# Band transposes of an attention kernel as 64-row halves, straight and crossed, among the row-tiled products

## The reference

```python
qkv = q @ in_proj_weight.T + in_proj_bias          # 16 heads of 16 features
scores = einsum('bhid,bhjd->bhij', qh / 4, kh)      # 1024 x 1024 for each head
rel = clip(pos[None, :] - pos[:, None], -64, 64) + 64
bias = take_along_axis(einsum('bhid,rd->bhir', qh / 4, rel_pe), rel)
attn = softmax(scores + bias)
x = layernorm(x + (attn @ vh) @ out_w.T + out_b)
x = layernorm(x + binarized_ffn(x))                 # 256 -> 1024 -> 256, exact gelu
```

## Time and profile before

| | us |
|---|---|
| median of 3 executions | 2435.11 (2433.6 to 2438.61) |
| the profiled execution | 2437.13 |
| its span, first to last instruction | 2435.4 |
| TensorE busy (products) | 2263.2, 93% of the span |
| VectorE busy | 1746.0, 72% |
| ScalarE busy | 1670.8, 69% |
| GpSimd busy | 966.1, 40% |

### The profile page before, as it was taken

How to read it: one execution, slowest core, us unless ns; L and a number is a source line. 1 busy time by engine, 2 the same in 40 slices (tenths; PEclk the granted TensorE clock), 3 DMA queues, 4 the chain that set the end, 5 groups by cost and what they waited for, 6 DMA issues and landing times. The chain is left out here.

```text
span 2435.4 us, 47764 instructions
## 1 busy us (share of the span) xinstructions
PE 2263.2 (93%) x14642; PEld 1272.1 (52%) x14642; DVE 1746.0 (72%) x3444; ACT 1670.8 (69%) x2239; POOL 966.1 (40%) x1565
## 2 busy tenths in 40 slices
PE   4998399999999999999999999999999999799997
PEld 3554144444444444444444444444444444688886
DVE  2454377777777777777777777777777773688885
ACT  2433157777777777777777777777777777466766
POOL 0000434444344443444334443444334432466663
PEclk9999579999999999999999999999999999899999
DMA  6998767777767777777777777777777762333311
GB/s 180 370 336 318 181 179 205 205 200 208 210 198 208 203 207 203 208 199 208 208 202 208 202 207 204 204 202 209 207 202 204 200 198 87 103 99 108 108 63 44
DMA packets 335292, 468.58 MB, mean 192 GB/s; under 512 B 90517, under 2 KB 263270, under 8 KB 335206
## 3 DMA queue, kind: packets, MB, share of 16 engines
q0 software_dynamic: 120960, 215.78, 35.0%
q1 hardware_dynamic: 201206, 243.05, 30.1%
q10 hardware_dynamic: 13040, 8.80, 1.2%
HBM read 244.73 MB, written 221.25 MB: 191 GB/s over the span
## 5 line engine op out<-in xcount | busy, mean ns | idle before, releaser
L896 ACT ACTIVATE probs<-weigh_ps 128x1024 f32<-128x1024 f32 x1024 | 1049.7, 1025 | 401.3 <-PE weigh_ps L1062 398.1
L1022 PE MATMUL ring_ps<-keys,queries 48*128 48x512 f32 x2048 | 839.3, 473 | 39.1 <-DVE partial_max L937 20.6
L948 DVE CUSTOM_DVE_ANT_1 ring_ps<-ring_ps,band_all 128x512 f32<-128x512 f32 x1008 | 681.0, 716 | 265.2 <-PE ring_ps L1022 265.0
L1062 PE MATMUL weigh_ps<-queries,keys 50*128 50x512 f32 (+3 forms) x2688 | 751.9, 385 | 1.4 <-ACT probs L896 0.8
L937 DVE TENSOR_REDUCE partial_max<-ring_ps 128x2 f32<-128x1024 f32 x512 | 627.9, 1226 | 165.7 <-PE ring_ps L1022 111.4
L1022 PEld LDWEIGHTS ring_ps<-keys,queries 48*128 48x128 f32 x2048 | 370.6, 187 | 517.9 <-issue 394.6
L1079 PE MATMUL sum_ps<-probs,values 128*32 128x512 f32 x4096 | 546.6, 605 | 0.1
L1047 PE MATMUL weigh_ps<-ident,band_all 128*128 128x128 f32 x2048 | 362.8, 290 | 22.8 <-ACT carried L884 20.2
L1062 PEld LDWEIGHTS weigh_ps<-queries,keys 50*128 50x128 f32 x2688 | 356.5, 186 | 17.7 <-ACT probs L896 9.5
L790 POOL DMA_DIRECT2D band_all<-band_scr x320 | 231.1, 725 | 332.9 <-DMA band_scr<-carried 318.3
L884 ACT ACTIVATE carried<-weigh_ps 128x512 f32<-128x512 f32 x512 | 302.6, 592 | 63.5 <-PE weigh_ps L1010 51.1
(11 more groups left out here) (115 smaller groups left out, 1858.6 us busy)
## 6 DMA issues: line engine op xcount, KB each, us to landing
band_scr<-carried SPq DMA_DIRECT2D x256, 512.0 KB, 4.0
band_all<-band_scr POOLq DMA_DIRECT2D x128, 512.0 KB, 6.6
band_all<-band_scr POOLq DMA_DIRECT2D x128, 256.0 KB, 3.3
keys<-k_scr POOLq DMA_DIRECT2D x128, 240.0 KB, 9.7
k_scr<-k_parts SPq DMA_DIRECT2D x16, 1792.0 KB, 8.4
q_scr<-q_parts SPq DMA_DIRECT2D x16, 1024.0 KB, 6.4
queries<-q_scr POOLq DMA_DIRECT2D x128, 128.0 KB, 2.9
o_scr<-weighted_s SPq DMA_DIRECT2D x64, 256.0 KB, 9.1
```

The source lines that it names most:

```text
L896: nc.scalar.activation(probs[:, u % PROBS], weigh_ps[weigh_of["scores", at]][:], ACT.Exp).then_inc(s_pr, 1)
L948: nc.vector.tensor_tensor_reduce(out=both, in0=both, in1=bias, scale=1.0, scalar=LOWEST, op0=ALU.add, op1=ALU.max, accum_out=partial_max[: ...
L1022: nc.tensor.matmul(dst, query_rows(c, h, ROWS, tile * P, (tile + 1) * P), key_rows(c, h, ROWS, c0, c0 + 512), start=True, stop=True, tile_ ...
L1062: last = nc.tensor.matmul(weigh_ps[weigh_of["scores", at]][:, h, e0 * P:e1 * P], key_rows(c, h, QROWS, k0, k0 + P), query_rows(c, h, QROWS ...
```

## The change

A tile of the band is no longer transposed with all 128 rows of the array, but in two halves of 64 rows (queries). The weights are 64 rows by 128 keys, the moving operand is 64 x 64 of the identity, and a half fills 64 of the 128 query columns. The array's rows 0 to 63 first take head 0's upper half while rows 64 to 127 take head 1's lower half ("straight"); then they swap heads ("cross"). The crossed ones wait on a semaphore for the straight ones, and the scores' products wait for the crossed ones. Each wait is followed by an instruction that increments a counter (`s_passed`). The order on TensorE becomes: looks (m, 0), weighs (m, 0), band product, weighted values, [turn of the maximum], straight (m, 1), looks (m, 1), cross (m, 1), straight of the next pair's part 0, weighs (m, 1), cross of the next pair's part 0. The two looks now stand together ahead of the weighs. ScalarE copies the turned maximum after the band instead of at the pair's start.

```diff
@@ ScalarE
                 def pair(i, step, m):
-                    if turns_at(step, 2 * m):
-                        copy_turned(i, turn_index(step, 2 * m))
                     if step >= 0:
                         expo(i, step, m, 0)
                     if m == 1 and step > 0:
                         copy_sums(i, step - 1)
                     if bands_at(step, m):
                         copy_band(i, band_index(step, m))
+                    if turns_at(step, 2 * m):
+                        copy_turned(i, turn_index(step, 2 * m))
                     if step >= 0:
                         expo(i, step, m, 1)
@@ TensorE
-                def turn_bands(i, c, m, part):
...
+                def turn_bands(i, c, m, part, cross):
+                    if not 0 <= c < G or not near(m, part):
+                        return
+                    n = weighed(m)[part] // 2
                     at = position(c, m, part)
+                    if cross:
+                        pe.wait_ge(s_straight, turns_before(i, c, m, part))
+                        pe.sem_inc(s_passed, 1)
+                    elif weigh_before["scores", at]:
+                        wait_for(i, weigh_before["scores", at])
+                        pe.sem_inc(s_passed, 1)
+                    for tile in near(m, part):
+                        side, e = (n - tile) % NT, tile % QT
+                        for r in range(HG):
+                            h, r0 = (1 - r if cross else r), r * ROW_TILE
+                            last = nc.tensor.matmul(
+                                weigh_ps[weigh_of["scores", at]][:, h, e * P + r0:e * P + r0 + ROW_TILE],
+                                band[r0:r0 + ROW_TILE, c % SLOTS, tile // 2, h, tile % 2, side * P:(side + 1) * P],
+                                ident[r0:r0 + ROW_TILE, r0:r0 + ROW_TILE], is_transpose=True,
+                                start=(not cross and tile == near(m, part)[0]), stop=False, skip_group_check=True,
+                                tile_position=(r0, 0))
+                            if tile == near(m, part)[-1]:
+                                last.then_inc(s_cross if cross else s_straight, 1)
...
+                def weighs_of(i, c, m, part):
...
+                    if near(m, part):
+                        pe.wait_ge(s_cross, turns_before(i, c, m, part))
+                    else:
+                        wait_for(i, weigh_before["scores", position(c, m, part)])
+                    for h in range(HG):
+                        weigh(c, m, part, h)
                 def pair(i, step, m):
-                    if turns_at(step, 2 * m):
-                        turn_max(i, turn_index(step, 2 * m))
-                    if step >= 0:
-                        turn_bands(i, step, m, 0)
-                    products(i, step, m, 0)
+                    following = (step, m + 1) if m + 1 < NT else (step + 1, 0)
+                    looks_of(i, step, m, 0)
+                    weighs_of(i, step, m, 0)
                     if bands_at(step, m):
                         band_product(i, band_index(step, m))
                     lagging(i, step, m)
-                    if step >= 0:
-                        turn_bands(i, step, m, 1)
-                    products(i, step, m, 1)
+                    if turns_at(step, 2 * m):
+                        turn_max(i, turn_index(step, 2 * m))
+                    turn_bands(i, step, m, 1, False)
+                    looks_of(i, step, m, 1)
+                    turn_bands(i, step, m, 1, True)
+                    turn_bands(i, *following, 0, False)
+                    weighs_of(i, step, m, 1)
+                    turn_bands(i, *following, 0, True)
```

More of the change, by code:

```diff
@@ L661, in post_ln_block @@
                     for u in (2 * m, 2 * m + 1):
-                        if turns_at(step, u):
-                            occupy(("turn", turn_index(step, u)), 1)
+                        if u % 2 and turns_at(step, u - 1):
+                            occupy(("turn", turn_index(step, u - 1)), 1)
                         if looks_at(step, u):
                             n = look_index(step, u)
-                            look_heads[n] = (1, 0) if u % 2 == 0 and (m % 2 == 0) != turns_at(step, u) else (0, 1)
+                            look_heads[n] = (1, 0) if u % 2 == 0 and (m % 2 == 0) != turns_at(step, u - 2) else (0, 1)
                             slots = LOOK_SLOTS[m % 2][u % 2]
@@ L1032, in turn_max @@
                                         ident[:]).then_inc(s_turn, 1)
-                def turn_bands(i, c, m, part):
-                    at = position(c, m, part)
-                    u = weighed(m)[part]
-                    n, g = u // 2, u % 2
-                    if u < 2:
-                        pe.wait_ge(s_min[g][c % SLOTS], i * (16 * HG) + 16 * HG * (c // SLOTS + 1))
-                    wait_for(i, weigh_before["scores", at])
-                    for h in range(HG):
-                        first = True
-                        for e in range(QT):
-                            tile = g * QT + e
-                            side = (n - tile) % NT
-                            if side < 2:
-                                nc.tensor.matmul(weigh_ps[weigh_of["scores", at]][:, h, e * P:(e + 1) * P],
-                                                 band[:, c % SLOTS, tile // 2, h, tile % 2, side * P:(side + 1) * P], ident[:],
-                                                 is_transpose=True, start=first, stop=False, skip_group_check=True)
-                                first = False
+                TURNED = [(0, 0), (0, 1), (1, 0), (2, 0), (3, 0), (4, 0), (4, 1), (5, 0), (6, 0), (7, 0)]
@@ new lines, in near, with turns_before @@
+                def near(m, part):
+                    n, g = weighed(m)[part] // 2, weighed(m)[part] % 2
+                    return [g * QT + e for e in range(QT) if (n - g * QT - e) % NT < 2]
+                def turns_before(i, c, m, part):
+                    return cnt(i, HG * len(TURNED), HG * (c * len(TURNED) + TURNED.index((m, part)) + 1))
+                def turn_bands(i, c, m, part, cross):
+                    if not 0 <= c < G or not near(m, part):
+                        return
+                    n = weighed(m)[part] // 2
+                    at = position(c, m, part)
+                    if cross:
[16 more added lines that the diff above has]
+                                last.then_inc(s_cross if cross else s_straight, 1)
@@ L1056, in weigh @@
                     tiles = range(g * QT, (g + 1) * QT)
-                    first = not any((n - t) % NT < 2 for t in tiles)
+                    first = not near(m, part)
                     rights = sum(1 for t in tiles if n > t + 1)
@@ L1089, in lagging, with looks_of @@
                         weighted(i, step - 1, NT - 2 + m)
[L1091 to L1109 removed]
+                def looks_of(i, step, m, part):
+                    if looks_at(step, 2 * m + part):
+                        n = look_index(step, 2 * m + part)
+                        for h in look_heads[n]:
+                            look(i, n, h)
+                def weighs_of(i, c, m, part):
+                    if c < 0:
+                        return
+                    g = weighed(m)[part] % 2
+                    if m == 0:
+                        pe.wait_ge(s_min[g][c % SLOTS], i * (16 * HG) + 16 * HG * (c // SLOTS + 1))
+                    if near(m, part):
[4 more added lines that the diff above has]
+                        weigh(c, m, part, h)
+                def pair(i, step, m):
+                    following = (step, m + 1) if m + 1 < NT else (step + 1, 0)
+                    looks_of(i, step, m, 0)
+                    weighs_of(i, step, m, 0)
                     if bands_at(step, m):
```

13 lines of the change are left out of this document (2 added, 11 removed).

## The result

The changed kernel takes 2816.0 us (median of 4, 2810.55 to 2817.14) where the kernel before takes 2436.32 (2433.6 to 2438.61). The ratio is 1.1546 [1.153, 1.1562], 380 us more. The sign was forecast, the size was not: 2816 lies far above the 2540 forecast and above the range. In what follows, one execution of e4 (2943.36 us) and one of e8 (3820.24 us, at a mean granted clock of 0.52) were slow ones and are outside the ratios; of e4's only steps at full clock are read.

A forecast was written before the change was run, and what follows sets the result against it. A loop through ScalarE, 3.17 us a pair, was taken as the bound. Pair terms, turns and increments gave 29.1 us a step against 27.47: +1.65 x 61 = +101 us on 2437.1, forecast 2540 us, range 2452 to 2630.

The forecast's parts named there:

- the clock: Rival, 3%: with TensorE waiting more, the clock could fall to half speed, some 2 us more per pair, far over 3000.
- pair 1 to 2: From weighted values of pair 1 to those of pair 2, weighs behind the band's copy: 4.33 us against 3.94.
- The halves' pace: Transposes by halves: a pair of halves side by side takes 0.055 us, against 0.105 for one full transpose.
- The third rival: Halves don't pair up, or their loads set the pace: 0.105 a pair, about 2570; one by one, 2666; chance 19%.
- From the second weigh to the exponential: Start of the second weigh to start of ScalarE's exponential, in every loop: 0.43 us.
- Increments: Counter increments behind the 20 waits per step: 0.1 us per step for those on the loops.
- The turn of the maximum: Moves from under ScalarE's work to between weighted values and looks, twice a step: 0.25 us each, 0.50 together.
- Plain pairs: Five pairs of a step without an extra: between 3.28 and 3.41 us, taken as 3.37, against 3.17 before.
- loop C: Loop over two pairs through look, weighs, band's copy, straight halves and part 1's exponential: 6.82 us, 3.41 a pair.
- The open pairs: Pairs 0 to 1 and 4 to 5: the full run's 0.37 goes, the longer loop stays; 3.67 us each.
- The "wrong if" list: Wrong if plain pairs repeat at 3.1 or less, band's copy ends well before straight halves, or their wait exceeds 0.1.
- TensorE's own work is the bound: Rival, 9%: TensorE's array time sets the pace, so halves save 3.2 us per step, giving 2242 us.

The follow-up runs named there:

- e4: Changed kernel with whole 128-row transposes in place of the straight halves, nothing for the crossed ones, no increments behind waits; 2850.05 and 2943.36 us, step 33.35.
- e8: Kernel before with TensorE's steps written out and the halves put into its old order of looks and weighs; 2571.28 us, ratio 1.0544.
- e1: Changed kernel with TensorE's steps written out, no loop on that engine; 2712.35 us, ratio 1.1133.
- e7: e1 with the looks of pair 1's second part done four times, filling a TensorE wait; 2603.08 us, ratio 1.0678.
- e6: e1 without the counter increments behind the waits for straight and crossed halves; 2667.26 us, ratio 1.0941.
- e9: e6 with the next pair's straight halves behind part 1's weighs, the crossed ones between the next pair's looks and weighs; 2652.3 us, ratio 1.0883.
- e12: Kernel before with ScalarE's copy of the sums moved from pair 1 to pair 2, behind the turned maximum's copy; 2417.93 us, ratio 0.9926.

## Why the prediction was wrong

**The sum of the 380 us, as measured.**

| term | from | us |
|---|---|---|
| longer step at full clock | (30.14 - 27.47) x 61 | 163 |
| stalls at the loop's turn | the row of waits | 71 |
| work at half clock | the rest | about 146 |

The third term is a remainder, but e1 and e7 measure it: e1 loses 104 us, of which 71 are stall and 33 mostly the slow work behind it; e7 takes a further 109 by the clock alone. Together 142. What is left in e7 is 2603 - 2437 = 166 us, and (30.03 - 27.47) x 61 = 156 of these are the step; about 10 lie outside the steps. 2603 is inside the range of the forecast: the longer step alone would not have left it.

**The step that failed is the clock**, which got 3% with the reason "Straight pairs leave no gap over 0.8 us". The forecast's own sum held the gap: in pair 1 to 2 it has the straight ones 1.34 behind the looks, and two looks take 0.50, so the array stands still for 0.84. The rows of after show 0.86 (1.15 for the loads). So the length of the gap was right there in the sum and its effect was put at nothing; no row of before could tell what such a gap does, since that kernel has none. The price was also misread. An execution of e8 at a mean clock of 0.52 took 3820.24 us, so "far over 3000" is about right for a kernel that is slow throughout. Left out was the case in between, in which the clock falls and comes back: 109 us in this kernel without the stalls.

**What was never asked is the length of TensorE's loop body.** The change adds loads, products, waits and increments to it, from 1730 to 2106 instructions, and the sum has no term for it. By e1 that is 104 us, which on top of the 2540 alone would have led out of the range. Nothing in the earlier trace rows shows it. The count of instructions was there to be read; the 30 packets of the kernel before say only that its own body fits.

**The longer step was forecast in sign and in kind, and undersized.** 29.1 was put for 30.14, so of the +2.67 the sum had +1.65. By its parts:

- *The halves' pace*: four halves start at 1098.68 and the weighs 0.14 later, which makes 0.07 for a pair of halves with the 0.055 taken. The third rival (loads set the pace, 0.105 a pair) is refuted. The rule of the Trainium skill that was weighed there (TensorE: Matmul & The Clock Gate, LDWEIGHTS) is not: a load of a half takes 134 to 140 ns and one of a whole tile 138 to 141 in the traces, alike whatever the rows. What doesn't hold is that the halves' loads follow one another, since four of them start within 0.1 us. The prediction's 0.06 between loads of whole tiles was true of the first two of a run only; the next start 0.11 apart.
- *From the second weigh to the exponential*, a term of every loop: 0.43 put, by the earlier trace rows, where the second weigh starts 0.34 behind the first and takes 0.39. In the changed kernel the two weighs start together and take 0.50, and ahead of the exponential of part 1 the term is 0.51 to 0.56 in all eight pairs of the step. That is about 0.9 of the 1.12 us by which the eight pairs together exceed their forecast.
- *Increments*: 0.1 put, without a row for it, and 0.40 by e6. The parts of this list overlap, so they don't add up exactly.
- *Pair 1 to 2*: 4.33 put, 4.45 measured, and e9 shows that the mechanism was the right one.
- *The turn of the maximum*: 3.62 put, 3.57 twice.
- *Plain pairs*: 3.37 put, but 3.69 and 3.75 in two that have no extra. The rows of pair 3 to 4, beside the weighted values at 1074.20 and 1077.89:

```profile
1075.06 0.59 ACT L886 ACTIVATE carried<-weigh_ps 128x512 f32<-128x512 f32 x1
...
1075.80 0.28 PE L1062 MATMUL weigh_ps<-ident,band_all 64*128 64x64 f32 x2
...
1075.93 0.50 PE L1081 MATMUL weigh_ps<-queries,keys 50*128 50x512 f32 x2
...
1076.50 2.03 ACT L898 ACTIVATE probs<-weigh_ps 128x1024 f32<-128x1024 f32 x2 [0.84 <-PE weigh_ps L1081]
```

  The path is the forecast's loop C: the copy of the band is over at 1075.65, the weighs behind the straight ones start 0.28 later and the exponential 0.57 after them, where 0.215 (0.05 + 0.165) and 0.43 were put. The base was short as well: 3.17 was taken for every pair without an extra, but with it the eight pairs before add up to 27.22 and not 27.47, since those from 2 to 4 and from 5 to 7 took 6.43 and 6.50, not 6.34.
- *The open pairs*: 3.67 put, 3.75 and 4.06 measured. TensorE's wait for its own results, put at 0.2, is on the path here. In 4 to 5 the crossed ones start 0.46 behind the straight ones and the weighs 0.36 behind those, as in e8. In 0 to 1 the next pair's straight ones stand behind the crossed ones and start at 1094.16, though the band's copy was over at 1093.77. No run takes that wait out of the new order while it keeps the halves, so its share is not separated.

**The "wrong if" list** had a wait for the straight ones themselves of more than 0.1. In e8 and in pair 4 to 5 of the changed kernel the crossed ones start 0.46 behind the straight ones, which take 0.28. What is left is 0.18 or 0.19, part of it the increment.

**What held.** That a loop through ScalarE and not TensorE's own work is the bound: e12 gets faster by moving one copy on ScalarE, with TensorE's list as it was. And that the order of TensorE's list is where the loss begins: 5.9 us a step by e4, against 3.2 that the halves give back, increments and all. The profile to expect was right in kind (waits ahead of the straight ones in nearly every pair, 483 of them), but ScalarE's wait rose by 261 us, not 100, and both engines fell to 63% of the stage, not 72%; in a step at full clock they are at 70%.

## What to carry to other kernels

Before you price the waits of a change to an engine's list, count the instructions of its loop body. Beyond a size (here between 1730 and 1858 on TensorE) each turn of the loop stands still, and a change that saves array time can pay for it in instructions. Then look in your own sum for the pair in which TensorE would stand still for most of a microsecond. The price of such a wait is not its length but the slow stretch behind it; repeating some harmless product in it is a quick test of what the clock costs. Work that needs the result of the same engine's previous work wants something else between the two. And a wait at the head of a list holds up everything behind it, also what doesn't need it: its price is the delay of all of that work, not of the waiting instruction alone.

## What the runs showed of the hardware that was not expected

- A TensorE loop body of 1858 instructions stalls 14 times for 57.5 us in all, one of 1730 or 1698 doesn't stall; the instruction queue's packets go from 30 to 156. One packet arrives in each of the 56 stalls of four kernels, and TensorE goes on 1.5 to 1.9 us after its end.
- With a semaphore between, products that need the result of short transposes start 0.46 us (straight to crossed, with an increment) and 0.33 us (crossed to weighs) behind these, which take 0.28 us.
- A wait of TensorE's products of 0.86 us in a step of 30 us brought the mean clock of the stage from 1.00 to 0.91, and cost 109 us; filled with repeated products it cost nothing.
- Increments of a semaphore on TensorE's queue were free at 4 per pair under 1 us of weighted values, 0.06 us a pair at 8, and 0.65 us a pair at 12. Twenty a step ahead of the transposes cost 0.40 us (e6).
- Two row halves transposing side by side take about 0.07 us for a pair of 64 x 64 pieces, where a whole tile took 0.105. Two weighs of 512 columns side by side take 0.50 us; the second of two staggered ones took 0.39.
